# A Mamba-2 block and a feed-forward layer on one core: the order of work in the first two groups, and who computes the low parts of the feed-forward weights

## The reference, cut to what matters

```
x = u                                              # 16 x 256 x 256, float32
zxbcdt = x @ W_in                                  # 256 -> z 512 | x 512 | B 128 | C 128 | dt 8
xBC = silu(conv1d(xBC, 4 taps) + conv_b)
dt  = softplus(dt + dt_bias);  A = -exp(A_log)
y   = ssd(x*dt, A*dt, B, C, chunk) + x*D           # state space recurrence over 256 positions
y   = rmsnorm(y * silu(z)) * norm_scale
x   = layernorm(x + y @ W_out)
Wg, Wu, Wd = dequant(4-bit codes, scales)          # 2048x256, 2048x256, 256x2048
x   = layernorm(x + (gelu(x @ Wg.T) * (x @ Wu.T)) @ Wd.T)
```

## Time and profile before

| what | value |
|---|---|
| median of three executions | 956.86 us (954.81 to 960.31) |
| profiled execution, its own time | 955.87 us |
| its span | 954.1 us |
| mean granted clock of PE | 0.962 |
| PE busy | 853.1 us (89%) |
| DVE busy | 709.3 us (74%) |
| ACT busy | 546.9 us (57%) |
| POOL busy | 70.0 us (7%) |
| chain that ended last | PE 61%, DVE 14%, DMA 8%, issue 8%, ACT 5%, POOL 3% |

### The profile page before, as it was taken

The page is one execution under the profiler, slowest core; times in us unless marked ns, Lnnn a source line. Parts: engine busy times, 40 slices in busy tenths (PEclk is TensorE's granted clock), DMA queues, the critical chain, the costliest instruction groups (busy, mean ns, idle before and its releaser), DMA issues.

```text
span 954.1 us, 16326 instructions
## 1 busy us (share of the span) xinstructions
PE 853.1 (89%) x5476; PEld 743.2 (78%) x5476; DVE 709.3 (74%) x1600; ACT 546.9 (57%) x1002; POOL 70.0 (7%) x105
## 2 busy tenths in 40 slices
PE   4657746889999999999999999999999999999987
PEld 3336545878888878988888788887898788888887
DVE  6675957977687878796878778787869687857453
ACT  4543547645864577456755596457745775456232
POOL 2101000020002000110002000200011000100000
PEclk9767978999999999999999999999999999999999
DMA  4401133002400141013201230014101420130000
...
DMA packets 37578, 61.32 MB, mean 64 GB/s; under 512 B 3264, under 2 KB 25888, under 8 KB 37536
## 3 DMA queue, kind: packets, MB, share of 16 engines
...
## 4 chain that ended last, share of the span: by engine, by line
PE 61%; DVE 14%; DMA 8%; issue 8%; ACT 5%; POOL 3%; SPq 1%; DVEq 0%; POOLq 0%; ACTq 0%
DMA dec<-spread 5%; PE gate_bank L535 5%; PE mixer L535 5%; PE up_bank L535 5%; PE up_bank L537 5%; PE up_bank L536 4%; PE gate_bank L537 4%; PE gate_bank L536 4%; PE down L535 4%; PE mixer L537 4%; PE down L536 4%; PE down L537 4%; PE mixer L536 4%; PE mixer L602 3%; ACT dec L764 2%
## 5 line engine op out<-in xcount | busy, mean ns | idle before, releaser
L535 PE MATMUL down<-wd_hi,in_hi 128*128 128x256 f32 x512 | 144.4, 282 | 1.0 <-DVE in_lo L1062 1.0
L536 PE MATMUL down<-wd_lo,in_hi 128*128 128x256 f32 x512 | 143.1, 279 | 0.0
L537 PE MATMUL down<-wd_hi,in_lo 128*128 128x256 f32 x512 | 142.8, 279 | 0.0
L535 PE MATMUL gate_bank<-hT_hi,wg_hi 128*128 128x512 f32 (+1 forms) x288 | 113.8, 395 | 23.6 <-ACT act_sb L797 23.6
L931 DVE SCALAR_TENSOR_TENSOR xbc<-mixer,chan,xbc 128x510 f32<-128x510 f32 (+1 forms) x162 | 110.9, 684 | 26.6 <-ACT xbc L732 25.4
L1062 DVE TENSOR_TENSOR in_lo<-act_sb,in_hi 128x512 fp32r<-128x512 f32 (+1 forms) x144 | 90.0, 625 | 51.7 <-ACT in_hi L783 51.0
L783 ACT ACTIVATE in_hi<-act_sb 128x512 fp32r<-128x512 f32 (+1 forms) x144 | 82.7, 574 | 64.3 <-PE down L537 53.0
L1076 DVE SCALAR_TENSOR_TENSOR act_sb<-up_bank,act_sb 128x512 f32<-128x512 f32 (+1 forms) x144 | 90.3, 627 | 37.9 <-PE up_bank L537 19.3
L535 PE MATMUL up_bank<-hT_hi,wu_hi 128*128 128x512 f32 (+1 forms) x288 | 107.7, 374 | 5.6 <-DVE act_sb L1076 5.6
L797 ACT ACTIVATE act_sb<-gate_bank 128x512 f32<-128x512 f32 (+1 forms) x144 | 78.7, 547 | 50.7 <-PE gate_bank L537 50.1
L537 PE MATMUL up_bank<-hT_hi,wu_lo 128*128 128x512 f32 (+1 forms) x288 | 107.3, 373 | 0.0
...
## 6 DMA issues: line engine op xcount, KB each, us to landing
...
```

The costliest lines, as they stand in the source:

```text
L535: nc.tensor.matmul(dst, lh, rh, start=first, stop=False, skip_group_check=True)
L536: nc.tensor.matmul(dst, lh, rl, start=False, stop=False, skip_group_check=True)
L537: return nc.tensor.matmul(dst, ll, rh, start=False, stop=last, skip_group_check=True)
```

## The change

- The order of group FIRST: A moves ahead of z1, x2 and CB0, H0 ahead of z3 and XT0; W0 ahead of L1; XT1 stays behind Y0, and both stand behind W1.
- Group 0 has its own list, "second": the first slot is empty, so that unit 0 comes before x5. H0 stands in the seventh slot with L0, XT0, X0, W0 (before: in the sixth); L1, XT1 stand behind H1; L2, XT2, L3, XT3 one slot sooner.
- All tables of the weights are new. Chunk 12 moves to group FIRST (`BESIDE_FIRST = 13`).
- In group 0 the low parts are computed by PE and ACT too (take off, `lower`), through one PSUM bank; `rest` on DVE goes. A take-off of chunk c >= 13 waits for `lower(c-1)`.
- With two tiles per group the steps of the softplus start behind the taps of x4 and end in those of x0.
- The rounding of W_out on ACT stands behind x3 (before: x1), and so POOL's part starts later.
- SP: spreads of group 0 ahead of the scales of chunk 20 (before 22); load of the next uT ahead of chunk 14 as before, the copy of the residual and the load of u ahead of chunk 15.

```diff
 USES = {
-    "first": ["dt", "x4", "x5", "x0", "x1", "z0", "CB0", "A", "x2", "z1", "x3", "z2", "z3", "XT0", "Y0", "XT1",
+    "first": ["dt", "x4", "x5", "x0", "x1", "z0", "A", "z1", "x2", "CB0", "x3", "z2", "z3", "XT0", "Y0", "XT1",
...
 SLOTS = {
-    "first": [["x5", "x0", "x1", "z0", "CB0", "A", "x2", "z1", "x3", "z2", "z3", "XT0", "H0", "L0", "H1", "X0", "L1",
-               "W0", "X1", "Y0", "W1", "XT1", "Y1", "g0", "S0", "op0", "g1", "S1", "op1", "ln1", "ln2"], []],
+    "first": [["x5", "x0", "x1", "z0", "A", "z1", "x2", "CB0", "x3", "z2", "H0", "z3", "L0", "XT0", "H1", "X0",
+              "W0", "L1", "X1", "W1", "Y0", "XT1", "Y1", "g0", "S0", "op0", "g1", "S1", "op1", "ln1", "ln2"], []],
+    "second": [[], ["x5", "x0", "z0"], ["x1", "CB0", "CB1", "z1"], ["x2", "z2"], ["A", "x3"], ["z3"], ["H0",
+               "L0", "XT0", "X0", "W0"], ["Y0", "H1", "L1", "XT1"], ["X1", "W1"], ["Y1", "g0", "H2", "L2",
+               "XT2"], ["X2", "S0", "W2", "op0", "g1"], ["Y2", "H3", "L3", "XT3", "X3", "S1"], ["W3", "op1",
+               "g2"], ["Y3"], ["S2", "op2", "g3"], ["S3", "op3", "ln1"], ["ln2"]],
...
+BESIDE_FIRST = 13
+DECODE = {FIRST: {"win": [1], "x2": [2], "XT1": [3], "S0": [4]}, 0: {"x0": [5], 3: [6], "z3": [7]}}
+VALUE = {FIRST: {"win": [0, 1], "x5": [2], "x0": [3], "A": [4], "x2": [5], "L0": [6], "XT0": [7], "X1": [8], "g0":
+         [9, 10], "g1": [11], "S1": [12]}, 0: {0: [13], "x0": [14], "x1": [15], "CB0": [16], "A": [17,
+         18], "L0": [19], "H1": [20], "L1": [21], "L2": [22], "S0": [23]}}
+UPPER = {FIRST: {"win": [0], "x0": [1], "z0": [2, 3], "A": [4], "z3": [5], "W0": [6, 7], "W1": [8], "S0": [9],
+         "op0": [10], "op1": [11, 12]}, 0: {"x5": [13], 1: [14], "z1": [15], "x2": [16], 4: [17, 18],
+         "X0": [19], 7: [20], "g0": [21], "W2": [22], "g1": [23]}}
+TAKE_OFF = {FIRST: {"x4": [0], "x1": [1], "z0": [2], "x3": [3], "z3": [4], "H1": [5], "W1": [6], "Y0": [7], "XT1":
+         [8], "g1": [9, 10], "op1": [11], "ln1": [12]}, 0: {"x0": [13], "CB0": [14], "x2": [15], "x3":
+         [16], 4: [17], "X0": [18], "Y0": [19], "W1": [20], 9: [21], "XT3": [22], 13: [23]}}
+LOWER = {FIRST: {"z0": [0, 1], "x2": [2], "z2": [3], "L0": [4], "X0": [5], "Y1": [6, 7], "S1": [8, 9], "ln1": [10,
+         11], "ln2": [12]}, 0: {"z0": [13], "CB1": [14], 3: [15], "x3": [16], "H0": [17], "Y0": [18],
+         "H1": [19], "Y1": [20], "Y2": [21], "W3": [22], 14: [23]}}
...
 LINKS = {4: {...},
-         2: {("x5", 1): [3, 4, 5], ("x5", 2): [6, 7, 8], ("x5", 3): [9, 10, 11], ("x0", 1): [12, 13, 14],
-             ("x0", 2): [15, 16, 17], ("x0", 3): [18, 19, 20, 21]}}
+         2: {("x4", 1): [3], ("x4", 2): [4, 5], ("x4", 3): [6, 7], ("x5", 1): [8, 9, 10], ("x5", 2): [11, 12, 13],
+             ("x5", 3): [14, 15, 16], ("x0", 1): [17, 18], ("x0", 2): [19], ("x0", 3): [20, 21]}}
...
-SPREAD_FIRST, SPREAD_NEXT = 6, 22
+SPREAD_FIRST, NEXT_UT, KEEP_FIRST, SPREAD_NEXT = 6, 14, 15, 20
...
-            return (GB, UB, *OB)[c % 4]
+            return (GB, UB, *OB)[c % 4] if c < BESIDE_FIRST else OB[1]
...
                     if c >= 4:

-                        pe.wait_ge(wt_lo.sem, c - 3)
+                        pe.wait_ge(wt_lo.sem, c - 3 if c < BESIDE_FIRST else c)
...
             def prep(g, item):
                 for c in UPPER[g].get(item, ()):
                     upper(c)
-                for c in LOWER[g].get(item, ()) if kind_of(g) == "first" else ():
+                for c in LOWER[g].get(item, ()):
                     lower(c)
...
-                    dve.wait_ge((wt_rest if c - 2 < BESIDE_FIRST else wt_lo).sem, c - 1)
+                    dve.wait_ge(wt_rest.sem, c - 1)
...
-            def rest(c):
-                dve.wait_ge(wt_hi.sem, c + 1)
-
-                dve.wait_ge(wt_lo.sem, c)
-                upper, lower = prep_dst(c)
-                tt(lower, chunk_out(c), f32(upper), ALU.subtract).then_inc(wt_lo.sem, 1)
```

More of the change, by code:

```diff
@@ L46 @@
              ["S1", "op1", "ln1"], ["ln2"], [], [], []]}
-BESIDE_FIRST = 12
-DECODE = {FIRST: {"x1": [2], "XT0": [3], "g0": [4]}, 0: {"x5": [5], "x1": [6], "x3": [7]}}
-VALUE = {FIRST: {"x0": [2], "x1": [3], "x2": [4], "x3": [5], "XT0": [6], "L1": [7], "XT1": [8], "Y1": [9],
-                 "g0": [10], "op0": [11]},
-         0: {0: [12], "x0": [13], 1: [14], "z1": [15], "x2": [16], 3: [17], "z3": [18], 4: [19], 5: [20],
-             6: [21], "XT1": [22], "W1": [23]}}
-UPPER = {FIRST: {"x1": [2], "z0": [3], "z1": [4], "z3": [5], "XT0": [6], "X1": [7], "Y1": [8], "g0": [9],
-                 "op0": [10], "g1": [11]},
-         0: {"x0": [12], "z0": [13], "x1": [14], 2: [15], "z2": [16], "x3": [17], 4: [18], "XT0": [19], "X0": [20],
-             "Y0": [21], 7: [22], 8: [23]}}
@@ L63 @@
-TAKE_OFF = {"x5": [0], "x0": [1], "z0": [2], "x2": [3], "x3": [4], "z3": [5], "XT0": [6], "Y0": [7],
-            "g0": [8], "op0": [9], "g1": [10], "op1": [11]}
-LOWER = {FIRST: {"x1": [0], "z0": [1], "z1": [2], "x3": [3], "z3": [4], "XT0": [5], "X1": [6], "Y1": [7],
-                 "op0": [8], "g1": [9], "op1": [10], "ln1": [11]},
-         0: {"z0": [12], "x1": [13], 2: [14], "z2": [15], "x3": [16], 4: [17], "H0": [18], "W0": [19], "Y0": [20],
-             7: [21], 8: [22], "XT2": [23]}}
+BESIDE_FIRST = 13
@@ L72 @@
              ("x1", 3): [15], ("z1", 0): [16], ("x2", 1): [17], ("x2", 2): [18], ("x2", 3): [19], ("z2", 0): [20, 21]},
[2 rows of a table removed]
[2 rows of a table added]
 CUT = 1.5 * 2 ** 15
-SPREAD_FIRST, SPREAD_NEXT = 6, 22
+WOUT_AT = "x3"
+SPREAD_FIRST, NEXT_UT, KEEP_FIRST, SPREAD_NEXT = 6, 14, 15, 20
 def kind_of(g):
@@ L91, in stages @@
 def stages(g, units):
-    order, at, slots = [], 0, SLOTS[kind_of(g)]
+    order, at, slots = [], 0, SLOTS["second" if isinstance(g, int) and g == 0 else kind_of(g)]
     for n, slot in enumerate(slots):
@@ L495, in _ @@
                     spread_sums(0, range(0, 2))
-                if c == BESIDE_FIRST + 2:
+                if c == NEXT_UT:
                     load_uT(0)
+                if c == KEEP_FIRST:
                     sp.wait_ge(wt_lo.sem, BESIDE_FIRST)
@@ L677, in prep @@
             def prep(g, item):
-                for c in TAKE_OFF.get(item, ()) if kind_of(g) == "first" else ():
+                for c in TAKE_OFF[g].get(item, ()):
                     b = chunk_bank(c)
@@ L703, in _ @@
             mixer("x4", FIRST)
+            prep(FIRST, "x4")
             run_all(pe, any_mixer, ffn, prep)
@@ L819, in any_mixer @@
                 mixer(name, g)
-                if name == "x1" and kind_of(g) == "first":
+                if name == WOUT_AT and kind_of(g) == "first":
                     act.wait_ge(wout_in.sem, 16)
@@ L838, in _ @@
             nc.scalar.activation(win_hi[:, :, X0:B0], x_raw, ACT.Copy).then_inc(win_top.sem, 1)
-            upper(0)
+            prep(FIRST, "win")
             act.wait_ge(z_in.sem, 16)
@@ L845, in _ @@
             mixer("x4", FIRST)
-            upper(1)
+            prep(FIRST, "x4")
             run_all(act, any_mixer, ffn, prep)
@@ L1115, in value @@
                 if c >= 2:
-                    dve.wait_ge((wt_rest if c - 2 < BESIDE_FIRST else wt_lo).sem, c - 1)
+                    dve.wait_ge(wt_rest.sem, c - 1)
                 tt(chunk_out(c), code, scales[:, c % 2, :].unsqueeze(1).to_broadcast([P, 2, CW]),
                    ALU.mult).then_inc(valued.sem, 1)
-            def rest(c):
-                dve.wait_ge(wt_hi.sem, c + 1)
-                dve.wait_ge(wt_lo.sem, c)
-                upper, lower = prep_dst(c)
-                tt(lower, chunk_out(c), f32(upper), ALU.subtract).then_inc(wt_lo.sem, 1)
             def prep(g, item):
-                for c in LOWER[g].get(item, ()) if kind_of(g) != "first" else ():
-                    rest(c)
                 for c in VALUE[g].get(item, ()):
@@ L1140, in _ @@
             decode(0)
-            value(0)
-            value(1)
             dve.wait_ge(win_top.sem, 1)
@@ L1147, in _ @@
             tt(wdt[:, :, 1, :], bc_raw[:, :, DT0 - B0:], f32(wdt[:, :, 0, :]), ALU.subtract).then_inc(win_ok.sem, 1)
-            decode(1)
+            prep(FIRST, "win")
             dve.wait_ge(win_top.sem, 3)
```

## The result

The changed kernel took 926.58 us (median of 4 runs, 925.33 to 930.15), the kernel before 958.23 us in the 4 runs beside it: a ratio of 0.967, 95% interval 0.964 to 0.971, 31.7 us less. The profiled execution took 930.15 us, the slowest of the four, where that of before took 955.87: 25.7 us between the two traces. Of the runs with the rests on DVE and with the next inputs split ahead of ln1, one execution of four took 2884.59 and 2929.55 us, three times as long as the others, from a cause that is not known; their medians here leave it out.

The account below looks back on a forecast made before the run. Bound: the chain of waits between in-order queues up to the second F1, then PE. First group -9.2 us, second -15.4 (-11.8 - 7.5 + 1.8 + 2.1), sum -24.6: 931.3, forecast as 932 us; range 921 to 946.

Parts of the forecast that it names:

- The spread: Second group, the sums' trip through DRAM: issued at 117.1 us, not 128.8, so H0 starts 11.8 us sooner.
- H0 to Y1: Second group: 7.5 us gained, 25.5 to 18.0, from four `rest` gone, a 3.06 us DVE wait gone, one unit less.
- Rival E: More gained: no interlocks, Y1's products at full clock, shorter cold-clock waits behind the filled hole; 925 us, chance 0.1.
- Y1 to F1: End of each group's stretch: second group 1.8 us lost; first group 1.4 us gained, 19.5 us before.
- Up to A: First group, start to A: 4.6 us gained, the copy of the sums at about 25.4 us instead of 30.05.
- A to Y1: First group: H0 at 34.1 us, Y1's products ready at 54.1 instead of 61.9; 7.8 gained counted from the start.
- POOL's W_out part: First group, 2.96 us now beside CB0, x3, z2: taken as 0 on DVE, bounds 0 and 2.96.
- The low parts on TensorE: Second group: eleven take-offs add 13.1 to 22.7 us of PE; priced at nothing on the path.
- C: Second group's spread leaves near 128 us as before, so the 11.8 us gain goes; 944 us, chance 0.12.
- D: Slower: each of 11 chunks' round trips of 3.9 us is exposed in the second group; 974 us, chance 0.06.
- F: Both groups: the chain has another, unseen limit and gains cancel; 955 us, chance 0.06.
- B: PE becomes the second group's bound, 6.2 us less gained; 938 us, chance 0.2; PE idle above 20 us speaks against it.

Follow-up runs that it names:

- the two executions: Two profiled executions of the unchanged changed kernel: the first took 930.15 us, the second was profiled in a repeat measurement with median 926.43 us, ratio 0.968.
- the last run: Changed kernel with the next inputs split ahead of ln1 in the second group and ScalarE's lower(17) behind z3, not H0: 925.43 us, ratio 0.964.
- the two parts that add: Kernel before with only the second group's spread moved ahead of chunk 20's scales: 948.91 us; kernel before with only the first group's new lists: 945.90 us.

## Why the prediction was right, and where it was off

**The order of gains was right.** The spread was the second group's largest term. *The spread* was forecast to bring 11.8 us up to H0 and brought 10.3 and 10.8; the difference is SP's queue. The walk had the write 1.0 us behind the sums' copy, 35.7 behind F1; it left 1.5 behind the copy and 37.0 behind F1, after block 7 and the scales of 18 (103.29 and 103.66 in SP's rows). The stall of value(18), forecast at 1.5 inside the slack, is 1.65 (105.90 in DVE's rows), and DVE then stands 2.32 us for H0 where 3.6 were forecast. The runs with the spread alone and with the spread held back show the term from both sides: 8 us and 5.6 to 7.4 us of time for 10.8 and 6.9 us on the queue. So about three quarters or more of such a move arrive in the time; at 1 us (x5 ahead of unit 0) nothing could be seen.

**H0 to Y1** was forecast at 18.0 us and took 19.5 and 18.2. The list of waits was right; what spread the two executions is the clock behind H0. Rival E had set hopes on a filled hole ending the low clock. Over this whole step the granted clock was 0.77 before, 0.83 and 0.91 in the two executions, and 0.83 again in the last run: better, and not at an end, for TensorE still stands 3 to 5 us there. Little hangs on it: in the run with the spread one scale sooner the clock was 1.00 throughout, and H0 to Y1 took 18.1 us.

**Y1 to F1** was forecast at 1.8 lost and 2.1 for interlocks, and 3.2 and 2.7 were lost. Over the whole second group the prediction has -15.4, the traces -13.1 and -15.5.

**The first group was mis-sized**: 9.2 us forecast, 13.7 and 14.8 seen at F1. The way up to A was sized right, the two terms behind it were both too small:

- *Up to A*: 4.6 taken, 3.7 and 4.6 seen. A's copy was to come at 25.4 us and came at 26.31 and 25.41 (25.2 to 26.4 in the other runs with this first group, save that of W_out). The walk gave W_out's move no term of its own here; its run shows that without it 2.8 us of this would be lost.
- *A to Y1*: H0 lay 8.75 us behind A's copy (8.7 in the walk), value(6) did not wait for its scales any more (40.36), and W1 was done 21.6 behind the copy (21.7 in the walk), so the walk held up to there. But the walk had Y1's products start behind decode(3) and gave them 2.9 us, a choice between the two clocks; they ran beside decode(3), at the full clock, and DVE waited 0.69 us for them (52.46). 3.2 forecast, 5.7 and 6.2 seen.
- *Y1 to F1*: I priced the 1.69 us wait at the late take-off and wrote that ln2 still waits for POOL. In the old trace DVE waits three times for TensorE in this stretch, 4.5 us in all; in the new one the three are 1.3 us:

```profile
70.23 0.48 DVE L1014 SCALAR_TENSOR_TENSOR h_sb<-mixer,rms,h_sb 128x256 f32<-128x256 f32 x1 [1.05 <-PE mixer L537]
...
76.21 0.48 DVE L1014 SCALAR_TENSOR_TENSOR h_sb<-mixer,rms,h_sb 128x256 f32<-128x256 f32 x1 [1.76 <-PE mixer L537]
...
78.80 2.54 DVE L1056 TENSOR_SCALAR h_sb<-h_sb,mv,lnr 128x256 f32<-128x256 f32 x2 [1.16 <-POOL lnr L1169]
```

  Only the priced one stands behind a take-off. The other two are waits for the 12 products of each tile's output; the new list has one value more of DVE's in each of these places (0.6 us each), and they shrink to 0.15 and 0.73 (59.89 and 64.32; a third, of 0.42, is for the norm's sums). And ln2's two steps take 0.74 us where they took 2.54 beside POOL's split of the next inputs, since that now comes after them (66.91 and 67.70). 1.4 forecast, 4.3 and 4.0 seen. What ln2 gained x4 gives back: it waits 1.80 us for POOL behind the first F1, inside the step from F1 to A's copy, of which 0.9 us was left instead of 1.7.

**POOL's W_out part** was priced at 0 with bounds 0 and 2.96. It ran at 33.55, beside one silu of DVE that took 0.57 us where the next took 0.43: 0.15 us, and DVE stood behind ScalarE right after. The rule of the Trainium skill (SBUF — State Buffer, "SBUF: two separate sides") by which the sum would have been up to 1.5 us worse, cost a tenth of that here. At ln2, where the prediction did not look, 3.27 us became 1.38 when POOL had nothing to do: four steps of 0.35 us, and 1.9 us more beside 2.7 us of POOL. The Trainium skill (the same page and section) says that where a VectorE instruction needs the port pair that the two engines share, whichever of the two starts first holds it for a whole instruction; the longer steps agree in kind, and no run here shows the lock itself.

**The low parts on TensorE** were priced at nothing on the path, and with 11 take-offs PE's busy time rose 6.7 us where the bounds from the earlier trace rows were 13.1 and 22.7; at least in part that is because the rest of its work ran at a higher clock (0.91 against 0.85). Nothing on the path was nearly right in sum, and not at one place: take-off 18 stands on the chain, 3.97 us idle ahead of it and 2.3 us to the next product at the low clock. Moving it did not pay, for ScalarE's list is tied to it, and moving lower(17) instead did not show either, with TensorE at the low clock behind its new gap.

**The rivals.** C is refuted by SP's row, D by the medians, F by the two parts that add. B's price (938) lies 11 us above the median, but B is not refuted by the sign that the prediction named: PE idled 15.7 and 14.6 us between the F1s, below the 20 that were to speak against it. It took the run with the rests on DVE. E's band (918 to 926) ends 0.6 us below the median and mine (926 to 936) just holds it; so near the edge, that it was mine and not E's is luck. The forecast of 932 lay 5.4 us above the median: 4.5 to 5.6 of it is the first group up to F1, less the 0.8 that was lost from F1 to A's copy, and the rest is within what two executions differ by (the profiled one of before lay 1.0 us below its first median and 2.4 below the one measured beside the change).

What stays open: how much of the 10 us by the medians is due to the rests on DVE, as 3.3 of the 9.7 between two traces lie outside the group that the edit touches; and whether a list exists in which TensorE neither waits nor idles between H0 and Y0. No run tried smaller units there.
